# Token mixer with fp32 probabilities in half arrays and q, k loaded in stacked form

## What is computed

```python
def _L0_tok_ref(qkv):
    N, C, T = (32, 128, 512)
    ch = qkv.shape[1] // 3
    q, k, v = jnp.split(qkv, 3, axis=1)
    scale = 1.0 / np.sqrt(np.sqrt(ch))
    weight = jnp.einsum('bct,bcs->bts', q * scale, k * scale)
    weight = jax.nn.softmax(weight.astype(jnp.float32), axis=-1).astype(weight.dtype)
    return jnp.einsum('bts,bcs->bct', weight, v)
```

## Time and profile before

| | us |
|---|---|
| median of three runs | 2807.41 |
| lowest and highest | 2806.83, 2809.67 |
| the profiled execution | 2800.67 |
| its span | 2798.9 |
| token mixer in it | 0 to 784.8 |

### The profile page before, as it was taken

How to read it: one execution, slowest core, us unless ns; L and a number is a source line. 1 busy time by engine, 2 the same in 40 slices (tenths; PEclk the granted TensorE clock), 3 DMA queues, 4 the chain that set the end, 5 groups by cost and what they waited for, 6 DMA issues and landing times. The chain is left out here.

```text
span 2798.9 us, 53432 instructions
## 1 busy us (share of the span) xinstructions
PE 2316.2 (83%) x18020; PEld 1371.8 (49%) x18020; DVE 1936.9 (69%) x3306; ACT 1567.7 (56%) x2502; POOL 1111.3 (40%) x1093
## 2 busy tenths in 40 slices
PE   5877777666849898954899999689998699999998
PEld 2655555555736565632444444256665244444443
DVE  5766666666759998966744457467776788878873
ACT  3666666666835555545732246255554566666663
POOL 2545555455634444411410015133332455555552
PEclk8878888788979999976999999899999899999999
DMA  3222222222225121101211113322221111111101
GB/s 89 77 71 79 77 78 79 76 79 78 57 88 174 60 64 60 57 31 48 81 59 65 49 59 98 99 65 79 77 76 56 43 36 46 43 38 45 42 31 46
DMA packets 122042, 185.80 MB, mean 66 GB/s; under 512 B 20645, under 2 KB 47877, under 8 KB 121914
## 3 DMA queue, kind: packets, MB, share of 16 engines
q1 hardware_dynamic: 121914, 184.21, 21.2%
HBM read 116.78 MB, written 41.94 MB: 57 GB/s over the span
## 5 line engine op out<-in xcount | busy, mean ns | idle before, releaser
L295 DVE TENSOR_REDUCE tm_negmax<-tm_s 128x1 f32<-128x512 f32 x512 | 343.5, 682 | 244.2 <-PE tm_s L379 239.6
L208 POOL TENSOR_TENSOR tm_plo<-tm_prob,tm_phi 128x512 f16<-128x512 f32 x256 | 323.6, 1268 | 360.9 <-ACT tm_phi L251 360.8
L244 ACT ACTIVATE tm_prob<-tm_s 128x1024 f32<-128x1024 f32 x256 | 266.0, 1039 | 253.9 <-PE tm_s L389 252.7
L379 PE MATMUL tm_s<-tm_qk 96*128 96x512 f16 x512 | 228.3, 447 | 207.4 <-DMA tm_qk<-tm_xs 190.6
L1994 PE MATMUL f_part<-f_xhi,gu 128*128 128x512 f16 x704 | 270.0, 384 | 14.5 <-ACT f_firstg L1815 4.3
L1994 PE MATMUL f_part<-f_xlo,gu 128*128 128x512 f16 x704 | 269.2, 382 | 0.0
L2016 PE MATMUL f_pz<-dn,f_ghi 128*128 128x512 f16 x704 | 216.8, 383 | 27.1 <-ACT f_zc L1847 27.1
L389 PE MATMUL tm_s<-tm_qk 98*128 98x512 f16 x512 | 224.9, 439 | 3.6 <-ACT tm_prob L244 2.5
L1784 POOL TENSOR_TENSOR f_firstg<-f_firstg,f_secondg 128x512 f32<-128x512 f32 x88 | 148.6, 1689 | 198.3 <-DVE f_secondg L1890 198.3
L251 ACT CAST tm_phi<-tm_prob 128x512 f16<-128x512 f32 (+1 forms) x256 | 215.2, 841 | 0.0
L606 POOL CAST a_v<-a_qkv 128x128 f16<-128x128 f32 x64 | 18.6, 291 | 380.3 <-PE a_bankO L985 372.0
(11 more groups left out here) (214 smaller groups left out, 7089.2 us busy)
## 6 DMA issues: line engine op xcount, KB each, us to landing
tm_qk<-tm_xs SPq DMA_DIRECT2D x384, 64.0 KB, 2.6
tm_xqk<-in_x SPq DMA_DIRECT2D x64, 256.0 KB
a_hin<-h SPq DMA_DIRECT2D x64, 256.0 KB, 2.6
a_hres<-h SPq DMA_DIRECT2D x64, 256.0 KB, 2.7
h<-a_hout SPq DMA_DIRECT2D x64, 256.0 KB, 2.1
f_hin<-h SPq DMA_DIRECT2D x64, 256.0 KB, 3.1
f_hres<-h SPq DMA_DIRECT2D x64, 256.0 KB, 2.8
tm_xv<-in_x SPq DMA_DIRECT2D x32, 256.0 KB
```

The source lines that it names most:

```text
L208: pool.tensor_tensor(plo[b][:, j, :], prob[b][:, j, :], phi[b][:, j, :], ALU.subtract).then_inc(plo_pool, 1)
L244: nc.scalar.activation(prob[b][:, 2 * h:2 * h + 2, :], s2[:, h, :, :], ACT.Exp, scale=SCALE).then_inc(exp_done, 1)
L295: nc.vector.tensor_reduce(negmax[u][:, m:m + 1], s1[:, m % 2, :], AX.X, ALU.max, negate=True).then_inc(max_done, 1)
L379: nc.tensor.matmul(s1[:, m % 2, :], qk[u][0:KS, 0, b, i * P:(i + 1) * P], qk[u][0:KS, 1, b, :], start=True, stop=True).then_inc(s1_ready, 1)
```

## The change

- The host lays out q and k three times over on 96 rows per tile (groups hi/hi, lo/hi and hi/lo need q or k each), and v already transposed. One load brings 96 rows of 16 KB.
- ACT casts all 96 rows to fp16; POOL then overwrites two blocks of 32 rows (k of group 1, q of group 2) with the low parts. The stacking DMAs are gone. A tile is split in two pairs of sequences.
- The maxima, too, go in two pairs per tile: two transposes of eight rows, two sets of two DMAs.
- Probabilities stay fp32 and are the moving operand (512 columns); v with 32 columns of ones is the weight (64 columns). The sequences of a pair write PSUM partitions 0 to 63 and 64 to 127. No casts of probabilities, no remainders, no transposes of v or of the result.
- The result comes out with channels on partitions, and the denominator on a partition of its own. ACT copies sums to SBUF, SP reshapes the two denominator rows to 128x16, DVE inverts, SP writes them to DRAM and reads them back repeated over the partitions, POOL multiplies, SP stores.
- First scores have three PSUM banks in place of two, shared with the transposed maxima; `LEAD` is 14, counted from tile n.

New data path on SP:

```diff
+            def load(t, u):
+                    wait_alone(sp, sp_passed, xlo_done, 4 * (t - 1))
+                    sp.dma_start(xqk[u][:, :, :, :].rearrange("p s b t -> p (s b t)"),
+                                 qk_dram[bass.ds(t * KS, KS)]).then_inc(qk_in[u], 16)
...
+            def maxima(t, u, pair):
+                    wait_alone(sp, sp_passed, s1_read, use(t + pair, turned(pair)) + 1)
+                    for part in range(2):
+                        sp.dma_start(qk[u][KS + part:KS + part + 1, 0, 2 * pair:2 * pair + 2, :]
+                                     .rearrange("o b (i t) -> o (b i) t", i=NT),
+                                     mrow[pair][:, part, :]).then_inc(mrow_in[pair], 16)
+            def denominators(t, u):
+                    wait_alone(sp, sp_passed, nd_done, 2 * t + 2)
+                    wait_alone(sp, sp_passed, rden_done, t - 1)
+                    sp.dma_start(dens[u][:, :], nd[u][C::2 * C, :, :].rearrange("q p (a e) -> q (p a) e", e=E))\
+                        .then_inc(dens_in[u], 16)
+            def inverses(t, u, half):
+                    wait_alone(sp, sp_passed, rden_done, t + 1)
+                    wait_alone(sp, sp_passed, rows_in[u], 16 * half)
+                    sp.dma_start(rden_dram[u].rearrange("b (a e) -> (b a) e", e=E), rden[u][:, :])\
+                        .then_inc(rden_out[u], 16)
+            def inverse_rows(t, u, half):
+                    wait_alone(sp, sp_passed, rden_out[u], 16 * (half + 1))
+                    wait_alone(sp, sp_passed, norm_done, t - 1)
+                    sp.dma_start(rows[u][:, :, :].rearrange("p b t -> p (b t)"),
+                                 rden_dram[u].unsqueeze(1).broadcast_to([2, 2 * C, 2 * T])).then_inc(rows_in[u], 16)
...
             def step(k, u):
                 n = 2 * k + u
-                load(n + 4, u)
+                inverse_rows(n - 2, u, k - 1)
+                maxima(n, u, 1)
+                denominators(n - 1, 1 - u)
                 load_values(n + 1, 1 - u)
                 store(n - 2, u)
-                stack(n + 2, u, 0)
-                stack(n + 2, u, 1)
-                stack(n + 2, u, 2)
-                maxima(n + 1, 1 - u)
-                stack(n + 2, u, 3)
+                load(n + 3, 1 - u)
+                maxima(n + 1, 1 - u, 0)
+                inverses(n - 1, 1 - u, k + u - 1)
```

POOL and ACT:

```diff
+            def x_lo(t, u, pair):
+                    b = slice(2 * pair, 2 * pair + 2)
+                    wait(pool, xhi_done, 4 * t + 2 * pair + 2)
+                    if pair == 0:
+                        wait(pool, norm_done, t - 3)
+                    for part, g in ((1, 1), (0, 2)):
+                        x, split = xqk[u][g * C:(g + 1) * C, part, b, :], qk[u][g * C:(g + 1) * C, part, b, :]
+                        pool.tensor_tensor(split, x, split, ALU.subtract).then_inc(xlo_done, 1)
+            def normalise(t, u, half):
...
+                    pool.tensor_tensor(hn[u][:, :, :], nd[u][:, :, :], rows[u][:, :, :], ALU.mult)\
+                        .then_inc(norm_done, 1)
...
+                x_lo(n + 1, 1 - u, 1)
+                normalise(n - 2, u, k - 1)
+                x_lo(n + 2, u, 0)
...
+                for i in range(8):
+                    exps(n, i)
+                    if i < 2:
+                        x_hi(n + 1, 1 - u, k + u, 2 + i)
+                    if i == 1:
+                        sums_out(n - 1, 1 - u, 1)
+                    if i == 5:
+                        sums_out(n, u, 0)
+                    if i in (4, 5):
+                        x_hi(n + 2, u, k + 1, i - 4)
```

PE, with `MAXIMA_AT = {11: 0, 3: 1}` and `VALUES_AT = {7: 0, 11: 1, 15: 2, 3: 3}` (slot: pair of maxima, block of value sums):

```diff
+            def sum_values(t, u, half, r):
+                    pair, h = r // 2, r % 2
...
+                    wait(pe, exp_done, 8 * t + 2 * r + 2)
+                    for j in (2 * h, 2 * h + 1):
+                        for q in range(2):
+                            b = 2 * pair + q
+                            last = nc.tensor.matmul(o[2 * C * q:2 * C * (q + 1), :], vt[u][:, j, :, b],
+                                                    prob[b][:, j, :], start=j == 0, stop=j == NT - 1)
+                    last.then_inc(pv_done, 1)
...
                 for g in range(SLOTS):
                     ahead, m = divmod(g + LEAD, SLOTS)
+                    pair = MAXIMA_AT.get(g)
+                    if pair is not None:
+                        maxima(n + 1 - pair, (u + 1 - pair) % 2, pair)
+                    scores_for_max(n + ahead, (u + ahead) % 2, m)
                     scores(n, u, g)
+                    r = VALUES_AT.get(g)
+                    if r == 3:
+                        sum_values(n - 1, 1 - u, k + u - 1, r)
+                    elif r is not None:
+                        sum_values(n, u, k, r)
```

More of the change, by code:

```diff
@@ L173, in maxima @@
[L173 to L179, removed]
+                    wait_alone(sp, sp_passed, norm_done, t + 1)
+                    for q in range(2):
+                        sp.dma_start(h_dram[bass.ds(t * P, P), :].rearrange("(p q c) t -> q c p t", q=2, c=C)[q],
+                                     hn[u][2 * C * q:2 * C * q + C, :, :]).then_inc(stored[u], 16)
@@ L324, in normalise @@
[L324 to L332 removed]
+                    p = place(m)
@@ L334, in step, with inverse_sums @@
+            def inverse_sums(t, u, half):
+                if inside(t, TILES):
+                    wait(dve, dens_in[u], 16 * (half + 1))
+                    wait(dve, rden_out[u], 16 * half)
+                    nc.vector.reciprocal(rden[u][:, :], dens[u][:, :]).then_inc(rden_done, 1)
             def step(k, u):
@@ L362, in _ @@
             pe.wait_ge(ident_in, 16)
-            pe.wait_ge(ones_set, 6)
-            def values_transposed(t, u, half):
-                if inside(t, TILES):
-                    wait(pe, v_in[u], 16 * (half + 1))
-                    wait(pe, norm_done, 2 * t - 1)
-                    for j in range(NT):
-                        last = nc.tensor.transpose(vT[:, j, :], xv[u][:, j * P:(j + 1) * P], ident[:, :])
-                    last.then_inc(vt_ready, 1)
-            def scores_for_max(t, u, half, m):
+            pe.wait_ge(ones_set, 4)
@@ L380, in scores_for_max, with maxima @@
                                      qk[u][0:KS, 1, b, :], start=True, stop=True).then_inc(s1_ready, 1)
+            def maxima(t, u, pair):
+                if inside(t, TILES):
+                    p = turned(pair)
+                    wait(pe, s1_read, use(t, place(HALF * pair + HALF - 1)) + 1)
+                    nc.tensor.transpose(s1[0:HALF, p % BANKS, 0:P], negmax[u][:, HALF * pair:HALF * (pair + 1)],
+                                        ident[:, :]).then_inc(s1_ready, 1)
             def scores(t, u, g):
@@ L406, in sum_values @@
-                    out = sums[b // 2][:, b % 2, i, :]
-                    rows = slice(i * P, (i + 1) * P)
-                    nc.tensor.matmul(out, prob[b][:, 0, rows], v[u][:, b, :], start=True, stop=False)
-                    for j in range(1, NT):
-                        hi, lo = phi[b][:, j, rows], plo[b][:, j, rows]
-                        nc.tensor.matmul(out, hi, vhi[u][:, j, b, :], start=False, stop=False)
-                        nc.tensor.matmul(out[:, 0:C], hi, vlo[u][:, j, b, :], start=False, stop=False)
-                        last = nc.tensor.matmul(out, lo, vhi[u][:, j, b, :], start=False, stop=j == NT - 1)
```

338 lines of the change are left out of this document (119 added, 219 removed).

## The result

The changed kernel takes 2891.57 us (median of four runs, 2889.42 to 2895.50), the kernel before beside it 2807.12 (2806.61 to 2809.67). The ratio is 1.030, interval 1.028 to 1.032: slower by 84 us, where 70 us less were forecast. The time lies above the range, too.

What follows compares the result with a forecast made beforehand. The denominators' round trip was to bound each tile: 6.0 us from slot 8 to the reciprocal, 2.8 for inverses to DRAM, 12.2 for rows, sum 21.0 against PE's 16.9. Forecast 2807.4 - 70 = 2737 us, range 2640 to 2822.

Steps and rivals of the forecast that it cites:

- What bounded the kernel before: Mixer, 23.6 us per tile: PE works 14 us, waits 7 for late stacking DMAs, loses 3 to slow clock.
- Issued about a tile and a half before its use: hidden: The q, k load on SP: 1.57 MB at some 400 GB/s takes 3.9 us and costs no tile time.
- Rival (d): PE's clock falls in the new waits: 22.7 us per tile, 2792 us; chance 0.07.
- In pieces of at most 2.4: PE waits some 4 us per tile in such short pieces; the clock had fallen only after some 5 us idle.
- The circle of the denominators: Round trip from PE's slot 8 through reciprocal, DRAM and repeated rows to the next slot 8: 21.0 us, the bound.
- The main term: Inverse rows read back from DRAM on two engines at 25.5 GB/s each: 524 KB in 10.3 us.
- Overlap of the halves: PE's fp32 products for a pair's two sequences work at once: block of four 2.1 us, otherwise 3.4.
- (b): PE's halves run in turn and PE bounds: 23.1 us per tile, 2805 us; chance 0.15.
- (c): PE's halves run in turn with fp32 weight loads uncovered: 24.1 us per tile, 2838 us; chance 0.14.
- the order of issue binds: PE's value block: outputs and weights are disjoint, so only strict issue order limits overlap, five steps of 0.43 us.
- Rival (a): Inverse rows use all engines, a chain from the block at slot 11 bounds: 18.6 us per tile, 2650 us; chance 0.13.

Runs made afterwards that it cites:

- the filled kernel: Changed kernel with store last, q, k load over 128 partitions, and 16 discarded score products ahead of PE's wait for the second maxima: 2742.9 us, 0.975 of before.

## Why the prediction was wrong

**What bounded the kernel before** needed no repair, and the 93 us lie in the mixer, where the change is.

**"Issued about a tile and a half before its use: hidden"** is the step that failed, for a reason of place and one of size. Its use was the wrong thing to ask after. SP's step puts the load behind the store, which waits for the normalising, and puts maxima and inverses behind the load, on the load's engines. I had counted the queue behind the load at 0.9 us (inverses 2.8 in place of 1.9); it is 3.4 to 6.2 (landing after 4.9 to 7.65, alone 1.5). And its 3.9 us were taken from a transfer to 128 partitions, where 96 get some 240 GB/s, 6.5 us. I had ended the circle at slot 8 of PE and never closed the one that goes from the rows through POOL and SP's store back to the rows. What the runs showed in its place is the circle of 4.0 + 9.8 + 12.7 us, with the load in it. With both faults taken out, the time is 2805.1, 86 us below the changed kernel (the order alone gave 75, the width alone 32).

**Rival (d)**, the falling clock, had 0.07 and 22.7 us per tile. With the load out of the circle it is what happens: 23.3 us per tile with it, 21.0 without. "In pieces of at most 2.4" was the wrong reason against it: PE's wait came in one piece of about 4, and the grant had fallen after some 2 us of idling. The 5 us that I read from the earlier trace rows were no lower bound.

**The circle of the denominators** was right in kind. With order, width and clock as the prediction had assumed them, the period is 21.0 and the time 2742.9 against the forecast's 21.0 and 2737 (with a third more bytes and discarded products in it). That the two agree so well is partly luck: from slot 8 to the reciprocal I had 6.0 us and the filled kernel has 5.0, inverses to DRAM 2.8 against 2.3, and from the rows' issue to PE's next slot 8 12.2 against 13.7. The mixer, too, ends there at 727.8, not 714. The main term held: two engines and 53 GB/s for the rows, as the window of 426 to 428 above shows. The whole step from their issue to POOL's start is 12.8 us; I had 12.2 up to PE. That the rows are its largest part is shown by the 116 us that 16 engines give.

**PE.** The block was taken at 2.4 us with its change of shape. From the end of the last score's stream to the next score it is 2.0: score at 420.61 plus 0.22, next score at 422.85. Overlap of the halves held, 0.86 us per product fits with the 0.96 at most, and rivals (b) and (c) had no part in it. Only that "the order of issue binds" was wrong, without effect. Rival (a), rows on all engines, did not occur by itself; made so, it gives 2775.8, not the 2650 of the prediction, since the load stays in the circle. With the load out of it, it gives 2655.5 at 18.9 us per tile, where (a) had 2650 at 18.6, and 2628.5 with the wide load.

**POOL** met its estimates (2.12 for x_lo, 2.34 for 2.2). The first second score came at 31.1 us, not 22. The slow first loads are only a part of that: with wide loads it comes at 28.6 to 29.2. The rest stays open.

In sum: the change took some 5 us per tile of waiting for stacks away, as forecast, and put the load, the inverses behind it and the rows, 9.8 + 12.7 us, in series between one normalising and the next.

## What to carry to other kernels

In a strictly ordered issue queue, look for circles that leave the compute engines: write down for each wait in the queue what stands behind it, and follow these transfers until you are back at the wait. "Issued long before its use" says nothing about a transfer that others stand behind. When a wait of some 4 us per tile remains on PE, as here, price the fall of the clock behind it as a term of its own; filling such a wait with discarded products was worth 62 us where it lay on the bounding circle and nothing where it didn't.

## What the hardware showed unexpectedly

- Loads to 96 partitions move 230 GB/s, loads to 128 partitions 422 (4 to 12 us, loads alone), both at a mean DMA share of about 1. The load's packets of 16 KB cut to 4 KB gain nothing (2898.7 against 2891.6 us). Why 96 gets no three quarters wasn't tried.
- fp32 products into the two halves of the array overlap fully: 1.93 us for four in either order of issue, 1.92 for the two of one half.
- The granted clock fell from 1.00 to 0.50 after some 2 us of idling in one place (401.3 to 403.4 above), where I had read some 5 from the earlier trace rows, and came back after 5 us of work. In the changed kernel it fell after 4.7 us (434.0 to 438.7), and came back after some 7.
- Issuing the v load costs SP 0.41 to 0.47 us in every tile of the six kernels with rows on 16 engines, 1.9 us (median) in the changed kernel, and 6.7 us with the load last, where load and rows had been issued less than 9 us before. I hadn't counted that issuing itself can be held up:

```profile
424.56 6.73 SPq L181 DMA_DIRECT2D tm_vt<-in_vt  x1
```
